# Gate logits of groups 1 to 3 computed in the same products as base_w, 264 and 384 columns a tile, with the copies and two DVE steps around them reordered

## The reference

```python
def _L0_ffn_ref(x, gate_w, base_w, base_b, lora_A, lora_B):
    gate_logits = jnp.einsum('bsd,ed->bse', x, gate_w)
    weights, selected = jax.lax.top_k(gate_logits, K)          # E, K, R = 8, 2, 16
    weights = jax.nn.softmax(weights.astype(jnp.float32), axis=2).astype(x.dtype)
    result = jnp.einsum('bsd,od->bso', x, base_w) + base_b
    w_full = jnp.sum(jax.nn.one_hot(selected, E, dtype=x.dtype) * weights[..., None], axis=2)
    low = jnp.einsum('bsd,erd->ebsr', x, lora_A)
    lora_out = jnp.einsum('ebsr,eor,bse->bso', low, lora_B, w_full)
    return result + SCALING * lora_out
x = x + _L0_ffn_ref(_L0_cond_ref(x, cond_128, ...), ...)       # 8 experts, base_w
x = x + _L1_ffn_ref(_L1_cond_ref(x, cond_128, ...), ...)       # 9 taps, 4 experts, top 2
```

## Time and profile before

| | us |
|---|---|
| median of 3 runs (lowest, highest) | 184.35 (184.05, 185.23) |
| the profiled execution, its own time | 183.59 |
| its span in the trace | 181.9 |
| PE busy, share of the span | 174.1, 96% |
| DVE, ACT, POOL busy | 119.4, 84.4, 84.2 |

### The profile page before, as it was taken

The page is one execution under the profiler, slowest core; times in us unless marked ns, Lnnn a source line. Parts: engine busy times, 40 slices in busy tenths (PEclk is TensorE's granted clock), DMA queues, the critical chain, the costliest instruction groups (busy, mean ns, idle before and its releaser), DMA issues.

```text
span 181.9 us, 2988 instructions
## 1 busy us (share of the span) xinstructions
PE 174.1 (96%) x1079; PEld 157.9 (87%) x1079; DVE 119.4 (66%) x253; ACT 84.4 (46%) x186; POOL 84.2 (46%) x86
## 2 busy tenths in 40 slices
PE   7999999899999999999999999999999999989990
PEld 7987889798888999998889999988889999988970
DVE  1289796987995435987954336897756734578471
ACT  3786578648244176414351366415134653244021
POOL 8024519960588289830019199530007874434000
PEclk9999999999999999999999999999999999999997
DMA  6999000032001410000041000000140000000336
GB/s 180 305 364 382 22 0 2 5 122 109 0 0 51 146 39 0 4 0 0 0 168 67 0 2 0 4 0 0 62 169 4 2 0 4 0 0 2 115 115 231
DMA packets 6350, 12.15 MB, mean 67 GB/s; under 512 B 704, under 2 KB 1088, under 8 KB 6336
## 3 DMA queue, kind: packets, MB, share of 16 engines
q1 hardware_dynamic: 6192, 11.84, 18.3%
q10 hardware_dynamic: 144, 0.13, 0.3%
HBM read 7.77 MB, written 4.19 MB: 66 GB/s over the span
## 4 chain that ended last, share of the span: by engine, by line
PE 75%; DVE 17%; issue 3%; ACT 3%; POOL 0%; DVEq 0%; POOLq 0%
PE ps L909 18%; PE ps L911 17%; PE ps L910 17%; PE ps L985 5%; PE ps L931 5%; PE ps L902 3%; DVE xs L743 2%; DVE late L653 2%; PE ps L1073 2%; DVE xsl L645 2%; PE ps L946 2%; PE ps L1074 2%; DVE above L649 1%; PE ps L982 1%; DVE base_l L645 1%
## 5 line engine op out<-in xcount | busy, mean ns | idle before, releaser
L909 PE MATMUL ps<-base_h,xTh 128*128 128x512 f32 x64 | 26.1, 408 | 0.3 <-DVE base_l L645 0.3
L911 PE MATMUL ps<-base_h,xTl 128*128 128x512 f32 x64 | 25.2, 394 | 0.0
L910 PE MATMUL ps<-base_l,xTh 128*128 128x512 f32 x64 | 25.2, 394 | 0.0
L325 POOL TENSOR_TENSOR xTl<-xT_s,xTh 128x512 fp32r<-128x512 f32 x12 | 15.0, 1277 | 15.8 <-ACT xTh L409 15.8
L330 POOL TENSOR_TENSOR zl<-outb,zh 128x340 fp32r<-128x340 f32 x15 | 14.6, 974 | 13.7 <-ACT zh L434 13.6
L341 POOL TENSOR_TENSOR x1Tl<-x1T,x1Th 128x512 fp32r<-128x512 f32 x12 | 16.4, 1378 | 8.1 <-DVE lw L673 8.1
L702 DVE TENSOR_TENSOR outb<-ps,s_sb 128x340 f32<-128x340 f32 x16 | 8.2, 511 | 17.9 <-PE ps L911 12.7
L689 DVE SCALAR_TENSOR_TENSOR x1T<-ps,side_s,xT_s 128x512 f32<-128x512 f32 x16 | 12.0, 750 | 11.3 <-PE ps L911 11.3
L985 PEld LDWEIGHTS ps<-mixT,p 128*128 128x128 f32 x128 | 17.0, 191 | 1.4
L985 PE MATMUL ps<-mixT,p 128*128 128x128 f32 x128 | 17.0, 276 | 0.0
L434 ACT ACTIVATE zh<-outb 128x340 fp32r<-128x340 f32 x16 | 7.8, 488 | 17.3 <-DVE outb L702 12.6
(11 more groups left out here) (190 smaller groups left out, 469.1 us busy)
## 6 DMA issues: line engine op xcount, KB each, us to landing
xT_s<-in_xT_dram SPq DMA_DIRECT2D x16, 256.0 KB, 4.3
out_dram<-outb SPq DMA_DIRECT2D x16, 256.0 KB, 2.4
...
```

Source lines behind the costliest of these rows:

```text
L325: nc.gpsimd.tensor_tensor(xTl[:, c, :], xT_s[:, g % 2, c, :], xTh[:, c, :].bitcast(F32), ALU.subtract).then_inc(x_lo, 1)
L909: nc.tensor.matmul(dst, sh, mh, start=start and c == 0, stop=False)
L910: nc.tensor.matmul(dst, sh, ml, start=False, stop=False)
L911: last = nc.tensor.matmul(dst, sl, mh, start=False, stop=stop and c == n - 1)
```

## The change

- `lgw_s` gets a split copy too, laid ahead of the split base_w in `xw_h`, `xw_l` (648 columns a chunk): one more ACT copy (`lgw_hi`) and one more DVE subtraction (`lgw_lo`) of 544 columns, both before `logits(0, t)`.
- For g = 1 to 3, `x_logits` and its 16 fp32 products go. `x_first` multiplies the split x by columns 0 to 263 (the 136 logit columns and 128 of base_w), `x_base` by the other 384. ACT copies the first part with `xa_out` (264 columns, per tile), the rest with `p0_out` (384); `lgs` and `p0` are views of one tile `xp`. Group 0 keeps its form.
- Both halves of a tile use the same bank, so `x_base(g, t)` waits for `xa_out(g, t)`, and `x_first` needs the split x of its group and a free bank of 2 to 5. Group 0's split x moves to `x1Th`, `x1Tl`.
- On ACT, `x_high(1, c)` and group 0's `p0_out` and `lwT_high` move ahead of the copies of the taps and of b1; `xa_out(1, t)` stands behind all of `mix_place`; all `sums_high(0, t)` stand behind `p0_out(1, 3)`. In the loop `gate_exp(n)` moves ahead of `p0_out(n, 1)`.
- On DVE, `lwT_low(1)` moves ahead of `sums_low(0, 0)`; in the loop `mwT_low(p)` moves ahead of `logits(n, t)`. On POOL, `x_low(1, c)` moves ahead of two subtractions for layer 1's weights.
- On PE, `mix_logits(1, t)` moves ahead of a small product that sums weights (L1149), and `turn_lw(1)` ahead of all of `x_base(1, 3)`. In the loop, two tiles of `x_first` stand ahead of `taps` and two behind it, and `turn_mw` and `mix_logits` stand behind `x_base(n, 0)`.

```diff
@@ buffers @@
-        base_h = sb("base_h", [P, DC, D], F32R)
+        xw_h = sb("xw_h", [P, DC, WX], F32R)
+        base_h, base_l = xw_h[:, :, LG:WX], xw_l[:, :, LG:WX]
-        p0 = sb("p0", [P, TG, D])
-        lgs = sb("lgs", [P, TG, LG])
+        xp = sb("xp", [P, TG, WX])
+        lgs, p0 = xp[:, :, 0:LG], xp[:, :, LG:WX]
@@ ACT @@
+            def xa_out(g, t):
+                act.wait_ge(xa_mm, TG * (g - 1) + t + 1)
+                if t == 0:
                     act.wait_ge(lw_ok, g)
+                    act.wait_ge(y_mm, DC * (g - 1) + 1)
+                nc.scalar.activation(xp[:, t, 0:HX], ps[:, P0[t], 0:HX], ACT.Copy).then_inc(xa_ok, 1)
@@ ACT, loop @@
                 gate_exp(p, gate1, dif1_ok, ex1_ok)
+                xa_out(n, 2)
+                xa_out(n, 3)
                 p0_out(n, 0)
                 mwT_high(p)
+                gate_exp(n, gate0, dif0_ok, ex0_ok)
                 p0_out(n, 1)
                 bias_high(n)
-                gate_exp(n, gate0, dif0_ok, ex0_ok)
@@ DVE, loop @@
                 route1(p)
+                mwT_low(p)
                 for t in range(TG):
                     logits(n, t)
-                mwT_low(p)
                 route0(n)
@@ PE @@
+            def x_first(g, t, chunks=range(DC)):
...
+                    last = hi_lo(ps[:, P0[t], 0:HX], [(hi[:, c, cols(t)], lo[:, c, cols(t)])],
+                                 [(xw_h[:, c, 0:HX], xw_l[:, c, 0:HX])], start=c == 0, stop=c == DC - 1)
@@ PE, group 1 @@
-            x_logits(1, 0)
-            pe.wait_ge(bsum_lo, 1)
-            x_logits(1, 1)
+            for c in range(DC):
+                for t in range(TG):
+                    x_first(1, t, (c,))
             make_y(0)
+            for t in range(TG):
+                mix_logits(1, t)
...
-            x_base(1, 3, (0, 1))
             turn_lw(1)
-            x_base(1, 3, (2, 3))
+            x_base(1, 3)
@@ PE, loop @@
-                x_logits(n, 0)
-                x_logits(n, 1)
+                x_first(n, 0)
+                x_first(n, 1)
                 taps(p)
+                x_first(n, 2)
+                x_first(n, 3)
+                x_base(n, 0)
+                turn_mw(p)
                 for t in range(TG):
                     mix_logits(n, t)
-                x_base(n, 0)
-                x_base(n, 1, (0, 1))
-                turn_mw(p)
-                x_base(n, 1, (2, 3))
-                x_base(n, 2)
+                x_base(n, 1)
                 for c in range(DC):
                     experts1(p, c)
-                x_base(n, 3, (0, 1))
+                x_base(n, 2)
                 turn_lw(n)
-                x_base(n, 3, (2, 3))
+                x_base(n, 3)
```

More of the change, by code:

```diff
@@ L152, in sum_parts @@
         def sum_parts(i):
-            return (xsh, xsl) if i < G - 1 else (base_h[:, 0:2, :], base_l[:, 0:2, :])
+            return (xsh, xsl) if i < G - 1 else (xw_h[:, 0:2, 0:TOK], xw_l[:, 0:2, 0:TOK])
         xs_last = xT_s[:, 0, 0:2, :]
@@ L363, in _ @@
             bias_rows(1)
-            for c in range(DC):
-                x_low(1, c)
             pool.wait_ge(tap_hi, 1)
@@ L507, in _ @@
             base_high(1)
-            xl_out(0, 0)
+            xl_out(0)
             base_high(2)
             base_high(3)
-            xl_out(0, 1)
+            xl_out(1)
+            nc.scalar.activation(xw_h[:, :, 0:LG], lgw_s[:, :, :], ACT.Copy).then_inc(lgw_hi, 1)
             act.wait_ge(zero_ok, 1)
@@ L526, in _ @@
             nc.scalar.activation(row_w[:, :], ps[:, BSUM, :], ACT.Copy).then_inc(bsum_hi, 1)
+            for c in range(DC):
+                x_high(1, c)
+            for t in range(TG):
+                p0_out(0, t)
+            lwT_high(0)
             act.wait_ge(in_tap, 16)
@@ L530, in _ @@
             nc.scalar.activation(b1_h[:, :], b1T_s, ACT.Copy).then_inc(b1_hi, 1)
-            for t in range(TG):
-                p0_out(0, t)
-            lwT_high(0)
-            for c in range(DC):
-                x_high(1, c)
-            xl_out(1, 0)
-            xl_out(1, 1)
             for g in range(1, G):
                 mix_place(g)
+            for t in range(TG):
+                xa_out(1, t)
             bias_high(1)
@@ L552, in _ @@
             p0_out(1, 3)
-            sums_high(0, 2)
-            sums_high(0, 3)
+            for t in range(TG):
+                sums_high(0, t)
             for i in range(1, G - 1):
@@ L946, in mix_logits @@
+                pe.wait_ge(mix_ok, BT * (i + 1) if i < 2 else BT * G)
                 nc.tensor.matmul(ps[:, LGM[t // 2], lg_cols(t)], mixer(i, t), lgs[:, t, :],
                                  start=True, stop=True).then_inc(lg_mm, 1)
-            def x_base(g, t, chunks=range(DC)):
+            def x_first(g, t, chunks=range(DC)):
+                if chunks[0] == 0:
+                    if g == 1:
+                        pe.wait_ge(p0_ok, t + 1)
+                        pe.wait_ge(lgw_lo, 1)
+                    elif t == 0:
+                        pe.wait_ge(zo_ok, TG * (g - 1) - 1)
+                    elif t == 1:
+                        pe.wait_ge(s_ok, TG * (g - 1))
+                    elif t == 2:
+                        pe.wait_ge(ze_ok, TG * (g - 1))
+                    else:
+                        pe.wait_ge(zo_ok, TG * (g - 1))
+                hi, lo = x_parts(g)
@@ L950, in x_base @@
                 for c in chunks:
                     pe.wait_ge(x_lo, DC * g + c + 1)
+                    last = hi_lo(ps[:, P0[t], 0:HX], [(hi[:, c, cols(t)], lo[:, c, cols(t)])],
+                                 [(xw_h[:, c, 0:HX], xw_l[:, c, 0:HX])], start=c == 0, stop=c == DC - 1)
+                if chunks[-1] == DC - 1:
+                    last.then_inc(xa_mm, 1)
+            def x_base(g, t, chunks=range(DC)):
+                first = HX if g else LG
+                hi, lo = x_parts(g)
+                for c in chunks:
@@ L962, in x_base @@
+                    last = hi_lo(ps[:, P0[t], 0:WX - first], [(hi[:, c, cols(t)], lo[:, c, cols(t)])],
+                                 [(xw_h[:, c, first:WX], xw_l[:, c, first:WX])], start=c == 0, stop=c == DC - 1)
                 if chunks[-1] == DC - 1:
@@ L1107, in _ @@
             keep_busy(4, 2)
-            x_logits(0, 0, (0,))
+            x_logits(0, (0,))
             pe.wait_ge(att_ok, 1)
@@ L1151, in _ @@
             last.then_inc(pjsum_mm, 1)
-            for t in range(TG):
-                mix_logits(1, t)
             x_base(1, 0)
```

108 lines of the change are left out of this document (54 added, 54 removed).

## The result

| | before | after |
|---|---|---|
| median (lowest to highest), us | 184.2 (183.66 to 185.23, 6 executions) | 186.9 (185.59 to 188.33, 6 executions) |
| the profiled execution, its span | 183.59, 181.9 | 188.33, 186.6 |
| PE busy | 174.1 | 176.4 |

The ratio after to before is 1.0156, 95% interval 1.0115 to 1.0196: slower by 1.6%, where 184.4 us and no change were forecast. The profiled execution of after is the slowest of the six, 1.43 us over their median, so it shows the mechanism and overstates the size.

The account below looks back on a forecast made before the run. PE was taken as the bound (busy 96%), with DVE nearly level between 28 and 61 us. Up to layer 1 +0.78 us, two loop turns -0.74, sum +0.04: 184.4 us on the median, range 182.4 to 185.8.

Parts of the forecast that it names:

- Prices of the products: PE's products: 0.121 us for 264 columns, 0.175 for 384, saving 0.62 us a group, 1.86 in three.
- cost nothing, 0.7 at most: Added ACT copy and DVE subtraction at 13 to 20 us: free while both engines wait for PE, else 0.7 us.
- no wait: Before x_first(1): POOL's x_low(1, c) keeps ahead, a chunk every 1.3 us against PE's 1.46, so PE never waits.
- Step 1: Group 1's mixers: xa_out(1, t) comes only after mix_place(3), so PE loses 0.6 us before mix_logits(1).
- Step 2: Group 1's bias rows and route: bias_high(1) behind xa_out makes DVE's work 2.2 us later, lw done at 49.5.
- Step 3: Sums before make_y(1): late high parts and POOL beside DVE delay x1; PE stands 2.0 us, layer 1 0.78 later.
- three such steps: Evidence against rival A: three DVE steps beside POOL took 1.3 to 1.5 us in the earlier trace, without exception.
- PE stands 2.0 us: In make_y(1): PE wants the bank for its third chunk at 56.23, but x1 of group 1 comes at 58.27.
- The loop, 0.37 a turn: Each loop turn: 0.62 us saved less 0.25 of waiting gives 0.37, two turns 0.74.
- The wait forecast at 0.25: Before the last chunk of experts1 in the loop: PE stands 0.25 us for p0_out(n, 1), now behind gate_exp(n).
- C: Rival: POOL runs beside all the sums, PE stands 4.1 us in make_y(1), +2.1 in all, 186.4; chance 0.09.
- B: Rival: nothing waits, layer 1 begins 1.84 us earlier, the loop gives 1.24, 181.3; chance 0.11.

Follow-up runs that it names:

- e8_lgw: The changed kernel with DVE's added subtraction lgw_lo moved behind route0(0); 186.77 us, ratio 1.0094 to the kernel before.
- e1_keep: The changed kernel with 16 products of constants on PE ahead of the third chunk of make_y(1); 186.01 us, ratio 1.0111 to the kernel before.
- e7_gate: The changed kernel with ACT's p0_out(n, 1) ahead of gate_exp(n) in the loop; 186.61 us, ratio 1.0081 to the kernel before.
- e15_pool: The changed kernel with POOL's four x1_low(0, t) waiting for DVE's last low part of the sums; 188.36 us, ratio 1.0176 to the kernel before.
- e16_half: The changed kernel with six reorderings on ACT, DVE and POOL, plus two of POOL's four x1_low(0, t) behind DVE's last sums_low; 182.69 us, ratio 0.9891 to before.

## Why the prediction was wrong, point by point

- **Prices of the products: right.** In after, 24 products of 264 columns take 2.91 us (76.81 to 79.72), 0.121 each, and 12 of 384 columns 2.11 (86.02 to 88.13), 0.176.
- **"cost nothing, 0.7 at most" for the added subtraction, and "no wait" before `x_first(1)`: wrong, and the first step that failed.** I had DVE waiting for PE at 13 to 20 us; its timeline in before shows it at work from 11.92 to 19.20, with 0.84 us idle ahead of `logits(0)`. The subtraction took 1.96 us beside POOL's of 680 columns (20.08 to 21.73), so `lb_l`, for which POOL's `x_low(1)` waits, ended at 28.8, and "no wait" became 0.64 us of idle time: `x_first(1)` begins 0.81 later behind `turn_lw(0)` than forecast. I had looked at what PE waits for and not at DVE's and POOL's own queues. e8_lgw confirms the place, and shows under it a wait of 0.32 for group 0's base copies, which I had not priced either. With some 0.5 in the products and `mix_logits(1)` behind it, group 1 reaches `make_y(1)` 1.32 later than forecast (1.3 and 1.2 in e1_keep and e7_gate, which change nothing ahead of it).
- **Step 1, 0.6 us lost before `mix_logits(1)`: right**, 0.49 with ACT's `xp` as releaser.
- **Step 2, `lw` 2.2 later than before: right in kind.** It was done at 52.07, 23.03 behind `turn_lw(0)` (predicted 49.5, 21.8): the lateness above and 0.4 more.
- **Step 3, the sums: right in mechanism and in the length of the standstill.** The first low part takes 1.57 (POOL beside it), and PE stands 2.07 where 2.0 was forecast. The chain is 1.2 to 1.5 us later behind `turn_lw(0)` than forecast, and PE 1.3, so that the length comes out the same. Two readings beside it were off, without weight in the sum: in before, DVE's last low part ends at 55.49 and not by 53.33, and of the "three such steps" in the earlier trace rows two stand there, the third being a sum of 1.33 us in the trace. Of the Trainium skill (SBUF — State Buffer, Who interferes with whom), the rule that I weighed here is borne out: e15_pool's 0.42 against 1.57 for the same instruction.
- **The sum took the standstill at its length: the second step that failed.** "PE stands 2.0 us" was to be followed by chunks at the usual 1.82; the third took 3.42 us. I treated the clock as constant because before shows 1.00 up to its last few us, but before never has PE idle for 2 us in this part. Four executions in six paid some 1.6 us.
- **The loop, 0.37 a turn: half right.** It was 0.23. The wait forecast at 0.25 before the last chunk costs 0.48 by e7_gate: from start to start 0.56 passed there (after, below) where 0.23 do, and something over 0.1 is lost elsewhere in the turn.

```profile
92.56 0.39 PE L1114 MATMUL ps<-mwT,b_l 128*128 128x512 f32 x1
93.12 0.50 PE L1113 MATMUL ps<-mwT,b_h 128*128 128x512 f32 x1 [0.18 <-ACT xp L442]
```

- **Rivals.** C had nearly the time (186.4), by luck: POOL did not run beside all the sums, and C has no fall of the clock in it. B's state, nothing waits, comes nearest in e16_half; it gave 182.69 where I had worked out 181.3. Its turns are as B has them (38.80 and 38.77; B's 39.47 less 0.62 is 38.85); its layer 1 begins 32.57 us behind `turn_lw(0)` and B's at 31.60, so 1 us of group 1 is still missing, 0.5 of it ahead of `x_first(1)`.

On the median: 1.3 for group 1, 0.2 for the standstill's own length, 0.3 for the loop, and of the clock 1.1 (1.6 us in two executions of three) make 2.9; missed were 2.5. The larger part is not the clock's: the two executions of after without a fall took 185.59 and 186.34 us, still 1.6 above the forecast on average.
